# Channel attention's sums inverted once each and repeated by DMA, with the next stage's first norm and turn placed in its last steps

## What is computed

```
# block five: q = layernorm(x), k = v = context, cut into 128 units of 8 rows, 256 columns
qk = einsum("bdm,bdn->bmn", qh, kh) / sqrt(8)
ret = einsum("bmn,bcn->bcm", softmax(qk), vh)
x = x + ret
# block six: xn = layernorm(x); weights rounded to three values, with scales
gate, up = split(xn @ wq_gate_up.T)
h = silu(gate) * up
x = x + rms_norm(h) @ wq_proj.T
```

## Time and profile before

| | |
|---|---|
| profiled execution | 748.16 us, span of its trace 746.4 us |
| median of three runs | 747.39 us (745.83 to 748.87) |
| PE busy | 608.7 us, 82% of the span |
| DVE busy | 463.2 us, 62% |
| ACT busy | 305.0 us, 41% |
| POOL busy | 235.9 us, 32% |
| chain that ended last | PE 57%, DVE 30%, issue 5%, ACT 3% |

### The profile page before, as it was taken

The page is one execution under the profiler, slowest core; times in us unless marked ns, Lnnn a source line. Parts: engine busy times, 40 slices in busy tenths (PEclk is TensorE's granted clock), DMA queues, the critical chain, the costliest instruction groups (busy, mean ns, idle before and its releaser), DMA issues.

```text
span 746.4 us, 12246 instructions
## 1 busy us (share of the span) xinstructions
PE 608.7 (82%) x4674; PEld 461.5 (62%) x4690; DVE 463.2 (62%) x966; ACT 305.0 (41%) x512; POOL 235.9 (32%) x251
## 2 busy tenths in 40 slices
PE   1563999958751699999785998977999999999993
PEld 1242556736640245566443666646999999999993
DVE  6999778787879898997767686958211111111110
ACT  4920255435674159888654556621111111111110
POOL 3321155255501598630412311101222222222211
PEclk9675799889985579999987999988999999999997
DMA  8000402200016316641303000024999999899952
GB/s 281 1 0 14 169 13 61 71 1 2 2 26 141 102 47 166 179 123 61 114 1 148 0 1 2 29 86 168 384 315 334 322 319 314 302 336 301 326 140 70
DMA packets 39594, 102.14 MB, mean 137 GB/s; under 512 B 6648, under 2 KB 31096, under 8 KB 35256
## 3 DMA queue, kind: packets, MB, share of 16 engines
q1 hardware_dynamic: 29312, 89.69, 35.9%
q0 software_dynamic: 4368, 5.90, 3.9%
q10 hardware_dynamic: 5856, 5.77, 2.2%
HBM read 87.45 MB, written 14.55 MB: 137 GB/s over the span
## 4 chain that ended last, share of the span: by engine, by line
PE 57%; DVE 30%; issue 5%; ACT 3%; POOL 2%; DMA 2%; POOLq 0%; DVEq 0%; SPq 0%; ACTq 0%
PE bank L1949 19%; PE bank L1962 9%; PE bank L1498 5%; DVE region L1225 3%; PE bank L1138 3%; PE bank L1098 2%; PE bank L580 2%; DVE XN L375 2%; PE bank L514 2%; PE bank L1122 2%; PE bank L1518 2%; DVE region L2240 2%; PE bank L2071 2%; DVE region L784 1%; PE bank L2078 1%
## 5 line engine op out<-in xcount | busy, mean ns | idle before, releaser
L1949 PEld LDWEIGHTS bank<-wide,region 128*128 128x128 f32 x1288 | 147.3, 192 | 2.5 <-ACT wide L1864 1.4
L1949 PE MATMUL bank<-wide,region 128*128 128x128 f32 x1288 | 148.0, 275 | 1.0 <-ACT wide L1864 1.0
L1830 DVE TENSOR_TENSOR wide<-wide,bank 128x512 f32<-128x512 f32 (+1 forms) x46 | 28.6, 621 | 124.6 <-ACT wide L1876 124.6
L1876 ACT ACTIVATE wide<-bank 128x512 f32<-128x512 f32 (+1 forms) x46 | 25.0, 544 | 181.9 <-PE bank L1949 181.9
L1225 DVE TENSOR_REDUCE region<-bank 128x2 f32<-128x512 f32 x128 | 80.2, 680 | 6.9 <-PE bank L1098 6.3
L1962 PE MATMUL bank<-region,wide 128*128 128x256 f32 x322 | 73.4, 379 | 0.7 <-DVE wide L1841 0.7
L1707 POOL DMA_INDIRECT residual_rows<-wide,to_row x23 | 36.4, 1581 | 105.5 <-DMA residual_rows<-wide,to_row 80.3
L1161 ACT ACTIVATE region<-bank 128x1024 f32<-128x1024 f32 x64 | 62.9, 1024 | 15.7 <-PE bank L1122 15.6
L1962 PEld LDWEIGHTS bank<-region,wide 128*128 128x128 f32 x322 | 59.4, 190 | 8.2 <-issue 1.0
L1098 PE MATMUL bank<-region 128*128 128x256 bf16 x256 | 51.8, 304 | 9.0 <-DVE region L1225 6.0
L389 POOL TENSOR_TENSOR rstd<-vareps,half_neg 128x4 f32<-128x4 f32 x16 | 17.4, 1085 | 114.6 <-DVE vareps L385 114.6
(11 more groups left out here) (316 smaller groups left out, 1145.4 us busy)
## 6 DMA issues: line engine op xcount, KB each, us to landing
region<-in_L_ffn_experts_dram SPq DMA_DIRECT2D x23, 1792.0 KB, 9.6
region<-in_L_ffn_experts_dram SPq DMA_DIRECT2D x23, 896.0 KB, 5.0
region<-ctx_parts SPq DMA_DIRECT2D x24, 192.0 KB
region<-norm_parts SPq DMA_DIRECT2D x24, 192.0 KB
channel_values<-wide ACTq DMA_DIRECT2D x8, 512.0 KB, 4.8
ctx_parts<-region SPq DMA_DIRECT2D x40, 64.0 KB, 2.0
region<-in_L_ffn_w_gate_up_dram SPq DMA_DIRECT2D x4, 512.0 KB, 5.3
wide<-channel_values SPq DMA_DIRECT2D x16, 128.0 KB, 2.6
```

Source lines behind the costliest of these rows:

```text
L1830: e.tensor_tensor(HB8[par][:, cols], silu8[:, cols], bank[hf][:, 512:512 + P * (hi - lo)], ALU.mult)\
L1949: last = e.matmul(bank[hf][:, at_:at_ + P], w[:, col:col + P], xbT[par][:, P * c:P * c + P], start=(c == 0), stop=(c == KC - 1))
```

## The change

The sums are loaded once each (16 x 256 values, laid out as 128 x 32 in `SUMS`) in place of eight times. DVE inverts 128 x 32. POOL writes the inverses to memory and reads them back with each row repeated eight times into `DEN5`; two transfers per tile on POOL's own queue. DVE inverts tiles 0 to 3 within the 64 steps (after steps 29, 37, 45 and 53). The norm of the first four tiles stands around the weight copies, PE turns them and weight group 3 eleven steps behind step 63, and DVE (not ACT) copies these out. In block six the second half's norm stands inside step 2, its turn after `gate_up(3)`, and `parts(3)` ahead of the wait for the last tile. In block eight the `busy` runs grow from 5 to 8 and from 3 to 5 matmuls.

```diff
 def values_in(e, i):
-            for dst, lo in ((NUM5, 0), (DEN5, DH)):
-                e.dma_start(dst[i % SETS], v[:, lo:lo + DH, :])\
-                    .then_inc(s_chan[f"values_in{i % SETS}"], 16)
+            e.dma_start(SUMS[i % SETS], v[:, DH, :].rearrange("a (b c) -> a b c", c=32)).then_inc(s_chan[f"values_in{i % SETS}"], 16)
+            e.dma_start(NUM5[i % SETS], v[:, 0:DH, :]).then_inc(s_chan[f"values_in{i % SETS}"], 16)
 def pe_channel(e, turn_half):
+            def first_half_T(w):
+                if w == PAIRS - 1:
+                    e.wait_ge(s_xn, 5 * NT + 4)
+                    e.wait_ge(s_tern["weights_T_ready"], 3)
+                    turn_half(XN, 0, 0)
+                    pe_weights_T(e, 3)
-                        (values, BEHIND + 2), (weights_T, 6)])
+                        (values, BEHIND + 2), (weights_T, 6), (first_half_T, 11)])
 def pool_channel_tiles(e, ch):
-            for i in range(NT):
-                add_values(e, ch, i)
-                if i == 3:
+            for first, n in ((0, 4), (4, 2), (6, 2)):
+                for w in range(n + 1):
+                    if w < n:
+                        inverses_out(e, first + w)
+                    if w >= 1:
+                        add_values(e, ch, first + w - 1)
+                    if w < n:
+                        inverses_in(e, first + w)
+                if first == 0:
                     pool_norm(e, 5, 0, 4)
+        def inverses_out(e, i):
+            e.wait_ge(s_chan["sums_inverted"], i + 1)
+            e.dma_start(inv_dram[i].rearrange("a (b c) -> a b c", c=32), SUMS[i % SETS]).then_inc(s_chan["inverses_stored"], 16)
+        def inverses_in(e, i):
+            e.wait_ge(s_chan["inverses_stored"], 16 * (i + 1))
+            e.dma_start(DEN5[i % SETS], inv_dram[i].unsqueeze(1).broadcast_to([P // DH, DH, D])).then_inc(s_chan["inverses_in"], 16)
 def vec_invert(e, i):
-            e.reciprocal(DEN5[i % SETS], DEN5[i % SETS]).then_inc(s_chan["sums_inverted"], 1)
+            e.reciprocal(SUMS[i % SETS], SUMS[i % SETS]).then_inc(s_chan["sums_inverted"], 1)
+        INVERT_AT = [TP5 * (i + 3) + 5 for i in range(4)]
 def vec_channel(e, ch):   # what stands behind the 64 steps now
+            e.wait_ge(x_done, 4 * NT + 4)
+            norm_variance(e, ch, 5, 0, 4)
+            for g in range(3):
+                weights_T(g)
+            norm_tiles(e, 5, 0, 4)
+            for i in range(4, 6):
                 vec_invert(e, i)
+            for c in range(KC):
+                e.wait_ge(s_turn, TURN["tern"] + c + 1)
+                e.tensor_copy(XT6[:, c, 0:512], ps(c)).then_inc(s_turned, 1)
+            weights_T(3)
 def vec_ternary(e, ch):
             def second_half(t):
+                if t == 2:
+                    norm_tiles(e, 5, 4, NT)
             def rest_half(t):
                 if t == 1:
+                    parts(3)
                     e.wait_ge(x_done, 5 * NT)
                     norm_variance(e, ch, 5, 4, NT)
-                    norm_tiles(e, 5, 4, NT)
 def pe_ternary(e, turn_half):
-            e.wait_ge(s_xn, 5 * NT + 4)
-            turn_half(XN, 0, 0)
-            tile_steps([(gate_up, 0), (hidden_T, 1), (project, 2)], second_half)
+            tile_steps([(gate_up, 0), (second_half, 0), (hidden_T, 1), (project, 2)])
 def pe_experts(e, turn_half):
-            busy(4, 5)
+            busy(4, 8)
-            busy(4, 3)
+            busy(4, 5)
```

More of the change, by code:

```diff
@@ L241, in program @@
         SETS = len(NUM5)
+        SUMS = [wide[:, N + 32 * j:N + 32 * j + 32] for j in range(SETS)]
         low5 = top[0]
+        inv_dram = nc.dram_tensor("channel_inverses", (NT, P // DH, D), F32, kind="Internal").ap()
         o_dram = nc.dram_tensor("channel_values", (NT, 4, P, D), F32, kind="Internal").ap()
@@ L1237, in maxima_parts, with inverses, weights_T @@
                     .then_inc(s_chan["maxima_split"], 1)
-            pair_steps([(maxima, 0), (maxima_parts, 1)])
-            for g in range(3):
+            def inverses(w):
+                if w in INVERT_AT:
+                    vec_invert(e, INVERT_AT.index(w))
+            def weights_T(g):
                 e.wait_ge(s_tern["weights_turned"], g + 1)
                 e.tensor_copy(t6_blocks()[g][0], ps(T6_BANKS[g]).bitcast(BF16)).then_inc(s_tern["weights_T_ready"], 1)
-            for i in range(4):
+            pair_steps([(maxima, 0), (maxima_parts, 1), (inverses, 0)])
+            e.wait_ge(x_done, 4 * NT + 4)
[4 more added lines that the diff above has]
+            for i in range(4, 6):
                 vec_invert(e, i)
+            for c in range(KC):
+                e.wait_ge(s_turn, TURN["tern"] + c + 1)
+                e.tensor_copy(XT6[:, c, 0:512], ps(c)).then_inc(s_turned, 1)
+            weights_T(3)
         def later(w, n):
@@ L1350, in hidden @@
             def hidden(i):
-                if i + 1 < NT:
+                if i + 1 < NT and i not in (2, 3):
                     parts(i + 1)
@@ L1359, in hidden @@
                         .then_inc(s_tern["hidden_ready"], 1)
+                if i == 3:
+                    parts(4)
             def mean_square(i):
@@ L1422, in act_ternary @@
         def act_ternary(e, leave_half):
-            leave_half(XT6, 0, 0, s_turn, s_turned, base=TURN["tern"])
-            for g in range(3, 6):
+            for g in range(4, 6):
                 e.wait_ge(s_tern["weights_turned"], g + 1)
@@ L1478, in pe_ternary @@
         def pe_ternary(e, turn_half):
-            e.wait_ge(s_xn, 5 * NT + 4)
-            turn_half(XN, 0, 0)
             e.wait_ge(s_chan["probs_ready"], PAIRS)
+            e.wait_ge(s_tern["weights_T_ready"], 4)
             e.wait_ge(s_chan["values_copied"], 4 * NT)
-            for g in range(3, 6):
+            for g in range(4, 6):
                 pe_weights_T(e, g)
-            e.wait_ge(s_tern["weights_T_ready"], 6)
             def gate_up(i):
@@ L1503, in hidden_T @@
                 e.wait_ge(s_tern["hidden_ready"], 2 * i + 2)
+                if i == 0:
+                    e.wait_ge(s_tern["weights_T_ready"], 6)
                 if i >= 1:
@@ L1520, in project, with second_half @@
                 last.then_inc(s_tern["projected"], 1)
-            def second_half(t):
-                if t == 2:
+            def second_half(i):
+                if i == 3:
                     e.wait_ge(s_xn, 6 * NT)
@@ L1865, in rows_T @@
                 if s == 0:
-                    e.activation(silu8[:, 0:1], ident[:, 0:1], ACT.Silu).then_inc(s_moe["silu_table"], 1)
-                    e.wait_ge(s_moe["silu_table"], 1)
+                    ch.link(e.activation(silu8[:, 0:1], ident[:, 0:1], ACT.Silu))
             def gate_silu(s, par):
@@ L2126, in _ @@
             pe_f8(e)
-            pe_channel(e)
+            pe_channel(e, turn_half)
             pe_ternary(e, turn_half)
@@ L2187, in _ @@
             act_batch(e)
[L2188 removed]
+            act_experts(e, ch, leave_half)
         @block.vector
```

19 lines of the change are left out of this document (7 added, 12 removed).

## The result

The changed kernel takes 733.84 us in the median of four runs (732.65 to 737.28), beside it the kernel before 746.85: a ratio of 0.9825 (95% interval 0.9802 to 0.9849). The forecast was 736.3, with 732.0 to 742.0 as its range. The profiled execution took 732.65 us (span 730.9), 15.5 less than that of before.

A forecast was written before the change was run, and what follows sets the result against it. PE, idle in two holes, was taken to bound the kernel. `gate_up(4)` 11.3 us earlier, less 0.2, gave 11.1 off the profiled 748.16, 737.1; with that execution 0.77 above the median, 736.3, range 732.0 to 742.0.

The forecast's parts named there:

- The bound: PE through blocks five and six: two holes in its work; the change is worth how much earlier `gate_up(4)` starts, 11.1 us.
- First hole: PE ahead of `gate_up(0)`: it starts at 370.1 instead of 376.49 and ends at 375.2 instead of 383.32, gaining 8.1 us.
- rival E: Early turn only swaps a norm wait for later exponentials, or DVE's loop waits for loads: half left, about 742; chance 0.06.
- The inversion: DVE within the 64 steps: 128 x 32 takes 0.3 us (bounds 0.20 and 1.63), with no wait entering the loop.
- The round trip: POOL's transfers of an inverse: 2.6 out, 2.9 in, 0.3 of semaphores, 5.8 us; bounds 4.5 and 18.2.
- Rival B: POOL and DVE hinder each other: a return leg waiting for `parts(3)` comes up to 1.7 us later, 738.0; chance 0.12.
- the page that I weighed: Skill's figure for a POOL transfer, about 2.0 us plus bytes over 436 GB/s: round trip 4.3 us, time 734.8.
- Second half: Block six: tile 2's product starts 9.2 us earlier, then 13.6 to `gate_up(4)` instead of 15.67; `gate_up(4)` at 407.3, not 418.60.
- The fillers and the second slot: Block eight's longer fillers before the second slot's gather wait: worth 0, ends -0.6 (shorter logits) and +1.7 (clock falls).
- The sum: Whole kernel: profiled 748.16 less 11.1 is 737.1; a timed run should read 736.3.
- A: Slow trip, both legs at the gather's median of 5.1 us, 10.2 in all: 740.7; chance 0.12.
- C: Slower than before: worst legs, 18.2 us, give 768; gain gone from a trip of about 11.5; chance 0.04.

## Why the prediction was right

**The bound.** That the change is worth how much earlier `gate_up(4)` starts held up to the second slot: about 12.6 us after R, 13.0 at the slot. Forecast were 11.1. From the slot on, the clock takes 1.4 back.

**First hole, 8.1 us.** Measured from R: `gate_up(0)` starts about 6.7 earlier (forecast 6.4) and ends 8.4 earlier at the full clock (forecast 8.1). The runs show its parts: with full inversions in the new places `gate_up(0)` comes 128.8 after R, 3.1 earlier than before, and the small form adds about 3.6 by keeping the loop short. The early turn is worth 1.6 at `gate_up(0)`, and by the ratios (0.9876 and 0.9825) nearly 4 us of the time, with what the clock and the second slot's wait add behind it; how much of that addition belongs to the turn isn't shown. It is not the nothing of rival E, by which it only swaps one wait for another.

**The inversion, 0.3 us, no wait in the loop.** 0.34, and no wait. Full inversions there took 1.74 each, the upper bound's size.

**The round trip, 5.8 us.** 5.2 for the last tile; the first tile's trip took 7.8, since its store landed late. The rounds of the first four took 3.8, 5.1 and 3.8 (forecast 4.7) and ended at 342.3, far ahead of the norm's need, so an error there cost nothing. For the last tile my estimate stood between two effects that I had not split: the transfers alone take 4.55, and 0.65 is the return's place behind tile 6's addition. Rival B was right to that extent, not by a lock on the transfer but through POOL's add, which took 1.60 beside DVE; the return itself landed in 2.21 with the casts of `parts(3)` on DVE all the while. By the page that I weighed (the Trainium skill, DMA: Bandwidth & Descriptors, Anatomy of one DMA — SWDGE (gpsimd) path) the trip is about 4.3, an estimate; the trace agrees with it where the return isn't queued, 4.55.

**Second half.** Tile 2's product starts about 10.3 earlier after R (forecast 9.2): the inversion came about 0.5 sooner than in the sum, trip and addition were about 0.4 shorter, the variance 0.2. From the product to `gate_up(4)` the forecast had 13.6 and it took 13.3 (388.81 to 402.11), but by another path, so that this agreement is in part luck. The sum let `gate_up(3)` and the turn run beside DVE's work, where "even at a half clock they hardly show". In after the chain goes through them: `gate_up(3)` at a clock that is half at first, then the copies of the turn, then `hidden_T`; with the turn late, `gate_up(3)` took 1.16 longer, and `gate_up(4)` came later by that too. Where `gate_up(3)` kept the full clock (both inversions together, and tiles 6 and 7 in full), the chain does go through DVE's terms, and from product to `hidden_T` it took 9.06 both times, instead of 9.62 (388.81 to 398.43). So the fallen clock costs about 0.6 here, and the terms of the sum were about 0.8 too long: 12.8 from product to `gate_up(4)` with both inversions together (390.07 to 402.87). The hole of about 4 us before `gate_up(3)` is 3.85. What the sum did not tell is which edit brings this part: it spoke of the last tile being done earlier, and the order alone does it (42.1 us from `gate_up(0)` to `gate_up(4)` without it, as before).

**The fillers and the second slot, 0 with +1.7 as an end.** Here the forecast took the wrong end: the slot lost 1.62 on its matmuls, 1.4 by the end of the span. The mechanism named, a longer gap and a fallen clock, is what the trace shows; that the fillers bring it about is refuted, since the old counts lose the same. In before, and in the run with the new form alone (a wait of 1.32), the slot kept its clock; with the moves it fell in every run but one. Which of their differences decides is not settled.

**The sum.** From R on, the profiled runs differ by 11.6, the forecast's 11.1 with two errors of opposite sign (1.9 more up to the second slot, 1.4 less from there); that they nearly cancel is luck. By the ratio, 0.9825 of the 747.39 shown before is 734.3, 2.0 under the forecast; the interval's ends are 732.6 and 736.1, and the forecast lies just above them. So the gain was put a little too small. Rivals A and C fall with the trip of 5.2, and the longest, 7.8, stays under their 10.2 and 11.5.

## What to carry to other kernels

A cheaper form that needs a transfer pays only where something else hides the transfer: alone it made this kernel 1.4% slower, and with its transfers under the 64 steps it turned a gain of 1.2% into one of 1.75%. When a hole is left behind a chain, look at where the first link is issued, not only at the links: moving one 0.34 us inversion a tile step forward, and its transfers with it, was worth 3 us, while moving the work behind it only carried the wait to the next place. Before two profiles are subtracted, compare a row of unchanged code ahead of the change: here 3.9 of 15.5 us lay there.

## What the runs showed of the hardware

Plain transfers on POOL's queue were mostly quicker than the gathers and scatters of the earlier trace rows (medians of 5.1 and 8.4 us). For the last tile it was 1.70 us to store 16 KB and 2.21 to 2.24 to read back 128 KB, each with 0.54 us of POOL's own time to issue (0.82 for the first store). All sixteen of after, and POOL at the first of them:

```profile
DMA to landing us min/median/max: 1.7/2.2/5.1
```

```profile
320.35 0.82 POOL L1222 DMA_DIRECT2D channel_inverses<-wide  x1
325.75 0.58 POOL L1226 DMA_DIRECT2D wide<-channel_inverses  x1 [4.58 <-DMA channel_inverses<-wide]
```

Three were slow: two stores (5.4 and 4.4 us from issue to POOL's next instruction, at 320.35 and 355.46) and one return (3.7, at 333.35). Each was issued 0.2 to 1.0 us behind one of ACT's 512 KB stores (320.14, 354.80, 332.31), and the DMA engines were 0.7 to 0.9 busy in the two microseconds around it, against the 0.2 to 0.3 of the 20 us stretches from which the forecast judged them. That the big stores are the cause is likely but not shown; PE waited for none of the three.

POOL's addition of 128 x 256 takes 0.72 alone and 1.60 beside a DVE subtraction of 128 x 1024, which itself takes 1.82 there and 1.21 to 1.23 alone. The two take turns: in after POOL's multiply runs first (380.55 to 381.29), DVE's subtraction ends at 382.38, and POOL's add, started at 381.36, ends at 382.96, 0.6 behind it. The Trainium skill (SBUF — State Buffer, SBUF: two separate sides) calls the shared port an exclusive lock, not a split of bandwidth; the rows agree.

The same 56 matmuls of the second slot took 6.52 us after waits of 1.39 (before), 1.32 and 1.04 us, and 8.00 to 8.15 after 1.36, 1.63, 1.67, 1.87 and all longer ones, up to 3.35. The length of that wait alone does not tell which. The Trainium skill (TensorE: Matmul & The Clock Gate, Part 1) says that the window in which the chip looks at PE's activity runs freely and isn't started by the kernel's work, so that the same work can meet it differently; no run here isolates that.
